# First-layer projections on one Trainium2 core: from one 32-bit matmul to three 16-bit matmuls, with GpSimd writing the arrangements

## The chip, the cores and the metric

The kernel runs on one core of a Trainium2 chip. The metric is device time in microseconds (us) of one execution, as the median of several. The engines are named as the profile names them: PE (TensorE, matmuls), PEld (TensorE's weight loads), DVE (VectorE), ACT (ScalarE), POOL (GpSimd), SP (SyncE, which issues the DMAs).

## The reference, cut to what matters

The network has several layers on x of shape (8, 128, 32, 32). The change lies in the first, a window attention with shifts 0 and 2, two channel halves and a local position term:

```python
for s in SHIFTS:                                   # (0, 2)
    xs = jnp.roll(x, (-s, -s), axis=(1, 2)) if s > 0 else x
    for idx, (nh, hs, nw, ws) in enumerate(strip_params):
        xsp = xs[:, idx * sd:(idx + 1) * sd]
        qkv = jnp.einsum('bchw,oc->bohw', xsp, wq)
        q, k, v = (qkv[:, :sd], qkv[:, sd:2 * sd], qkv[:, 2 * sd:])
        lepe = _dwconv3(v, w_lepe, b_lepe)         # 3x3 depthwise, per channel
        ...
        ow = jnp.einsum('whqk,whkc->whqc', attn, vw) + lw
```

Its input is x after a group norm, and x is added to its result.

## The kernel before, in words

All of this is the stage `window_projections` (line 205 on), one call, between the group norm's statistics and the stage `window_attention`, which reads what this stage stores. The stages are separated by a barrier of all engines. Channels lie on the 128 partitions, and a position of an image is a column (N = 1024, HALF = 512). The function `images` (L236) makes every engine walk the 8 images in order, two buffer slots in turn; within an image `u` counts four units (two shifts by two directions of strips), and each engine's instructions stand in the order in which its function is written. What one engine hands another goes over semaphores that count up; `grant` gives the buffers' first credits.

- **DVE** prepares an image one ahead (`prepare`, L276 to L280): it normalises X into `xn`, repeats its first 64 columns at the end, and copies it into `xw`, the same positions in the order of the vertical strips.
- **PE** makes for each unit the scores' projections (L332: two matmuls of 512 columns into `qk_ps`, all queries and keys of the unit) and the values (L337: eight matmuls of 64 columns into `v_ps`, with a block of 128 positions of the image as the stationary operand). Even units read `xw`, odd ones `xn`. After the four units the image's local position terms are summed in `l_ps` (L346): values and 3x3 taps are folded into one matrix for each tap (`wt`, made by DVE at the start), so a term is a matmul on the padded image `xp`, shifted by the tap; `lepe_pieces` cuts them at the image's edges into 36 pieces, 18 of one row (32 columns), 9 of 512 columns and 9 of 416 to 480. All of these operands are 32-bit, and one 32-bit matmul stands in the trace as two MATMUL records, each with its weight load.
- **ACT** casts each `qk_ps` to 16 bit (`hl`, L310), copies `v_ps` out (L313), and after the four units pads the next image into `xp` (L303).
- **DVE** subtracts the cast from `qk_ps` to get the low 16-bit half (L286), and after `l_ready` adds `l_ps` and the bias sum `bsum` to X (L291).
- **SP** stores both halves with four DMAs for each unit (`store_stacks`, L201 and L202) and the values with one (L254). `hl`, `vs`, `qk_ps` and `v_ps` have two buffers each: ACT may not write `hl` for a unit until the stores of the unit two before have landed (`hl_out`), and PE may not write `qk_ps` until DVE is through with the unit two before (`lo_done`).
- **POOL** does nothing in this stage.

At the stage's start SP loads the weights (L246) and the taps (L247); DVE waits for all five loads, makes `wt`, and only then normalises the first image.

The lines that the change and the prediction touch are those named above. `copy_scaled` (L360) is the copy by GpSimd, a multiplication by a column of ones.

Of the kernel before, what the change touches and what calls it, by code (L numbers as in the profile page):

```python
# [34 lines left out]
HALF = N // 2  # L35
D = 8
SHIFT = 16.0
STACK = 3 * D
ROWS = STACK + 2
MAX_UNIT = 32768.0  # L40
# [164 lines left out]
def window_projections(chip, X, mean_g, rstd_g, dram, qk_scr, v_scr):  # L205
# [4 lines left out]
    with chip.stage() as ctx:  # L210
# [6 lines left out]
        bsum = chip.buf(ctx, "bsum", [C, 1])  # L217
        scratch = chip.buf(ctx, "scratch", [1, 16])
        xn = chip.buf(ctx, "xn", [C, 2, N + 64])
        xw = chip.buf(ctx, "xw", [C, 2, N])  # L220
        xp = chip.buf(ctx, "xp", [C, 2, H, W + 2])
# [5 lines left out]
        w_loaded, weights, normed, padded, edge, strips = (chip.sem(s) for s in (  # L227
            "w_loaded", "weights", "normed", "padded", "edge", "strips"))
        qk_ready, hi_done, lo_done = (chip.sem(s) for s in ("qk_ready", "hi_done", "lo_done"))
        v_ready, v_copied, l_ready, l_added = (chip.sem(s) for s in ("v_ready", "v_copied", "l_ready", "l_added"))  # L230
        hl_out = [chip.sem("hl_out") for _ in range(2)]
        v_out = [chip.sem("v_out") for _ in range(2)]

# [8 lines left out]
        with nc.Block() as block:  # L242
            @block.sync
            def _(sp):
                for dst, name in ((wqk, "w0_qk"), (wv, "w0_v"), (wl, "w0_lepe"), (bl, "b_lepe")):
                    sp.dma_start(dst[:], dram[name]).then_inc(w_loaded, 16)  # L246
                sp.dma_start(taps[:].rearrange("p s t c -> p (s t c)"),  # L247
                             dram["lepe_taps"].to_broadcast([C, 2 * 9 * C])).then_inc(w_loaded, 16)
# [12 lines left out]
            def _(v):  # L261
                grant(nc, scratch, [(lo_done, 2), (v_copied, 2), (l_added, 1),
                                    (hl_out[0], 64), (hl_out[1], 64), (v_out[0], 16), (v_out[1], 16)])
                nc.vector.memset(xp[:], 0.0).then_inc(weights, 1)
                v.wait_ge(w_loaded, 16 * 5)
                nc.vector.tensor_scalar(wqk[:], wqk[:], SHIFT, None, ALU.mult).then_inc(weights, 1)
                for s in range(2):
                    nc.vector.tensor_tensor(wt[:, s], taps[:, s],
                                            wl[:, s].unsqueeze(1).to_broadcast([C, 9, C]), ALU.mult).then_inc(weights, 1)
                nc.vector.tensor_tensor(bsum[:], bl[:, 0:1], bl[:, 1:2], ALU.add).then_inc(weights, 1)  # L270
                v.wait_ge(weights, 5)
                nc.vector.tensor_tensor(wt[:, 2], wt[:, 0], wt[:, 1], ALU.add).then_inc(weights, 1)

                def prepare(i, slot):

                    nc.vector.tensor_scalar(xn[:, slot, 0:N], X[:, i, :], mean_g[:, i, :], rstd_g[:, i, :],  # L276
                                            ALU.subtract, ALU.mult).then_inc(normed, 1)
                    v.wait_ge(normed, i + 1)
                    nc.vector.tensor_copy(xn[:, slot, N:N + 64], xn[:, slot, 0:64]).then_inc(edge, 1)
                    nc.vector.tensor_copy(xw[:, slot].rearrange("p (n h w) -> p n h w", n=8, w=4),  # L280
                                          xn[:, slot, 0:N].rearrange("p (h n w) -> p n h w", n=8, w=4)).then_inc(strips, 1)
# [12 lines left out]
                prepare(0, 0)  # L294
                images(v, image)

            @block.scalar
            def _(act):
                act.wait_ge(weights, 1)

                def pad(i, slot):
                    act.wait_ge(normed, i + 1)
                    nc.scalar.copy(xp[:, slot, :, 1:W + 1],  # L303
                                   xn[:, slot, 0:N].rearrange("p (h w) -> p h w", h=H)).then_inc(padded, 1)

                def image(i, slot, last):
                    for u in range(U):
                        act.wait_ge(qk_ready, i * U + u + 1)
                        act.wait_ge(hl_out[u % 2], i * 128 + (u // 2 * 64 + 64))
                        nc.scalar.copy(hl[:, u % 2, 0], qk_ps[:, u % 2]).then_inc(hi_done, 1)  # L310
                        act.wait_ge(v_ready, i * U + u + 1)
                        act.wait_ge(v_out[u % 2], i * 32 + (u // 2 * 16 + 16))
                        nc.scalar.copy(vs[:, u % 2], v_ps[:, u % 2]).then_inc(v_copied, 1)  # L313
                    if not last:
                        pad(i + 1, 1 - slot)

                pad(0, 0)
                images(act, image)

            @block.tensor  # L320
            def _(pe):
                pe.wait_ge(weights, 6)
                def image(i, slot, last):
                    pe.wait_ge(strips, i + 1)
                    for u in range(U):
                        src = (xw if u % 2 == 0 else xn)[:, slot]
                        at = 64 if u == 3 else 0
                        if u == 1:
                            pe.wait_ge(edge, i + 1)
                        pe.wait_ge(lo_done, i * U + u + 1)  # L330
                        for c in range(2):
                            last = nc.tensor.matmul(qk_ps[:, u % 2, c * HALF:(c + 1) * HALF], wqk[:, u, :],  # L332
                                                    src[:, at + c * HALF:at + (c + 1) * HALF], start=True, stop=True)
                        last.then_inc(qk_ready, 1)
                        pe.wait_ge(v_copied, i * U + u + 1)
                        for w in range(8):
                            last = nc.tensor.matmul(v_ps[:, u % 2, w * 64:(w + 1) * 64],  # L337
                                                    src[:, at + w * C:at + (w + 1) * C], wv[:, u, :],
                                                    start=True, stop=True)
                        last.then_inc(v_ready, 1)  # L340
                    pe.wait_ge(padded, i + 1)
                    pe.wait_ge(l_added, i + 1)
                    for half in range(2):
                        pieces = lepe_pieces(half)
                        for n, (tap, kind, r, rows, r_in) in enumerate(pieces):
                            last = nc.tensor.matmul(  # L346
                                l_ps[:, r * W:(r + rows) * W], wt[:, kind, tap, :],
                                xp[:, slot, r_in:r_in + rows, tap % 3:tap % 3 + W],
                                start=(n == 0), stop=(n == len(pieces) - 1))
                    last.then_inc(l_ready, 1)  # L350

                images(pe, image)


# [1962 lines left out]
```

## Time and profile before

| | |
|---|---|
| time, median of 3 runs | 3906.41 us (3897.05 to 3911.96) |
| the profiled execution, its own time | 3902.64 us |
| its span in the trace, first to last instruction | 3900.8 us |
| mean granted TensorE clock over the span | 0.92 of full speed |
| busy over the span | PE 86%, DVE 70%, ACT 54%, POOL 26% |
| this stage in the trace | about 20 us to 300 us |

The profile is one execution taken by the hardware profiler. Times in its rows are microseconds from the start of the span, "x64" is a count of instructions, and the time in brackets is how long the engine had stood idle before and what released it. Matmuls overlap in the trace, so the time of one is not what it costs in a row of many: for that, the starts of two rows are subtracted. PEclk is the granted clock of TensorE as a share of its full speed.

### The profile page before, as it was taken

The numbers are of one execution on the slowest core, as the hardware profiler recorded it, in microseconds if no ns is written. First come the engines' busy times: TensorE is split into PE (matmuls) and PEld (weight loads), VectorE is DVE, ScalarE is ACT, GpSimd is POOL, SyncE is SP. The second block draws the span as 40 slices with busy tenths as digits, with TensorE's granted clock in tenths as the row PEclk, the third lists the DMA queues.
The fourth block names the chain that finished last, engine by engine and source line by source line (L and its number), as shares of the span: only waits on it lengthen the run. The fifth ranks groups of instructions, "written<-read, shape, count | busy, mean of one in ns | idle before, by whom it ended". The sixth has DMA issues, their size and how long they took to land. (4 is left out here: it accounts for less than half of the span.)

```text
span 3900.8 us, 68078 instructions
## 1 busy us (share of the span) xinstructions
PE 3362.7 (86%) x24815; PEld 1499.4 (38%) x24815; DVE 2734.7 (70%) x4437; ACT 2099.7 (54%) x2668; POOL 1000.6 (26%) x868
## 2 busy tenths in 40 slices
PE   6997778846779999999999999778987949999999
PEld 4664445523522222222222222163356734444444
DVE  3227767646479999999899999443449647777776
ACT  1224667711217777777777777633432325555555
POOL 0001343320000000000000000004420048888887
PEclk9997877868869999999999999979999859999999
DMA  4443555510320000000000100004410114323230
GB/s 149 129 130 85 114 119 117 106 20 0 118 79 16 21 18 25 16 22 21 21 22 16 27 16 16 11 11 151 151 48 0 45 46 114 100 81 101 89 93 27
DMA packets 137471, 243.06 MB, mean 62 GB/s; under 512 B 36776, under 2 KB 49232, under 8 KB 136720
## 3 DMA queue, kind: packets, MB, share of 16 engines
q1 hardware_dynamic: 137232, 239.79, 22.6%
q8 instruction: 160, 2.62, 0.3%
q14 instruction: 79, 0.65, 0.1%
HBM read 167.36 MB, written 56.62 MB: 57 GB/s over the span
## 5 line engine op out<-in xcount | busy, mean ns | idle before, releaser
L1075 DVE TENSOR_REDUCE mxv<-mx_ps 128x1 f32<-128x512 f32 x2048 | 1277.0, 683 | 90.1 <-PE mx_ps L934 71.9
L1050 ACT ACTIVATE PT<-st_ps 128x1024 f32<-128x1024 f32 x1024 | 997.1, 1022 | 297.5 <-PE st_ps L947 297.3
L934 PE MATMUL mx_ps<-KS,QS 24*128 24x512 f16 x2048 | 613.7, 394 | 113.8 <-DVE mxv L1075 96.4
L2024 POOL TENSOR_TENSOR hg<-u,gb 128x512 f32<-128x512 f32 x352 | 580.3, 1654 | 131.5 <-DVE u L1985 101.2
L961 PE MATMUL o_ps<-PT,VA 128*32 128x512 f32 x4096 | 550.9, 610 | 0.5 <-ACT PT L1050 0.5
L947 PE MATMUL st_ps<-QS,KS 26*128 26x512 f16 x2048 | 400.6, 388 | 9.2 <-ACT TX L1040 8.4
L669 DVE TENSOR_REDUCE mxv<-mx_ps 128x4 f32<-128x512 f32 x512 | 319.8, 684 | 122.4 <-PE mx_ps L544 118.1
L1985 DVE TENSOR_TENSOR u<-h_ps,s 128x512 f32<-128x512 f32 x352 | 243.1, 691 | 190.7 <-ACT s L1946 185.6
L1946 ACT ACTIVATE s<-h_ps 128x512 f32<-128x512 f32 x352 | 210.0, 596 | 284.0 <-PE h_ps L1901 284.0
L947 PEld LDWEIGHTS st_ps<-QS,KS 26*128 26x128 f16 x2048 | 96.5, 91 | 559.2 <-issue 481.6
L365 POOL TENSOR_TENSOR mt<-nm,less 128x16 f32<-128x16 f32 x64 | 13.8, 216 | 1113.9 <-DVE nm L1080 1113.9
L645 ACT ACTIVATE PT<-st_ps 128x1024 f32<-128x1024 f32 x256 | 253.0, 1030 | 72.4 <-PE st_ps L560 71.1
L1899 PE MATMUL h_ps<-xh,m_wh 128*128 128x512 f16 x704 | 268.5, 381 | 12.5 <-DVE xl L1968 8.9
L1900 PE MATMUL h_ps<-xl,m_wh 128*128 128x512 f16 x704 | 268.3, 381 | 0.0
L1901 PE MATMUL h_ps<-xs,m_wl 128*128 128x512 f16 x704 | 268.1, 381 | 0.0
L1974 DVE TENSOR_TENSOR hl<-hg,hh 128x512 f16<-128x512 f32 x352 | 257.3, 731 | 0.1
L934 PEld LDWEIGHTS mx_ps<-KS,QS 24*128 24x128 f16 x2048 | 142.7, 91 | 294.7 <-DVE mxv L1075 272.5
L365 POOL TENSOR_TENSOR VA<-VS,unit 128x512 f32<-128x512 f32 (+1 forms) x64 | 52.9, 826 | 646.1 <-DMA VS<-v 604.0
L1941 ACT CAST hh<-hg 128x512 f16<-128x512 f32 x352 | 214.8, 610 | 5.0 <-POOL hg L2024 4.8
L544 PE MATMUL mx_ps<-QK 24*128 24x128 f16 x2048 | 173.4, 245 | 34.5 <-DMA QK<-qk 18.3
L370 PE MATMUL st_ps<-KS,ident 128*128 128x512 f16 x512 | 201.2, 393 | 1.6 <-ACT PT L1050 0.9
L560 PE MATMUL st_ps<-QK 26*128 26x128 f16 x2048 | 118.0, 243 | 59.0 <-DMA QK<-mT 58.4
(237 smaller groups left out, 4747.2 us busy)
## 6 DMA issues: line engine op xcount, KB each, us to landing
gb<-g SPq DMA_DIRECT2D x64, 512.0 KB, 3.7
gb<-g SPq DMA_DIRECT2D x32, 1024.0 KB, 5.6
QK<-qk SPq DMA_DIRECT2D x128, 192.0 KB
qk<-hl SPq DMA_DIRECT2D x80, 256.0 KB, 3.3
RB<-d SPq DMA_DIRECT2D x48, 256.0 KB, 3.5
gb<-g SPq DMA_DIRECT2D x64, 192.0 KB, 5.7
qk<-hl SPq DMA_DIRECT2D x64, 128.0 KB, 3.2
v<-vs SPq DMA_DIRECT2D x32, 256.0 KB
```

The source lines that it names most:

```text
L645: nc.scalar.activation(PT[:, n % 2, 2 * a:2 * a + 2], st_ps[:, a], ACT.Exp, scale=SCALE).then_inc(st_free[a], 1)
L669: nc.vector.tensor_reduce(mxv[:, u % 2, j, n // 2 % 2, at:at + 4], mx_ps[:, slot].rearrange("p (w k) -> p w k", w=4), AX.X, ALU.max).then_ ...
L934: nc.tensor.matmul(mx_ps[:, use % 3, :], rows(QS, g // 2, j, STACK)[:, t * C:(t + 1) * C], rows(KS, g // 2, j, STACK)[:, half * HALF:(half ...
L947: mm = nc.tensor.matmul(st_ps[:, a, e], rows(KS, g // 2, 2 * a + e, ROWS)[:, kt * C:(kt + 1) * C], rows(QS, g // 2, 2 * a + e, ROWS)[:, g ...
L961: mm = nc.tensor.matmul(o_ps[32 * j:32 * j + 32, :], VA[:, g // 2 % 2, kt, j, :], PT[:, n % 2, j, :], start=(kt == 0), stop=(kt == KT - 1))
L1050: nc.scalar.activation(PT[:, n % 2, 2 * a:2 * a + 2], st_ps[:, a], ACT.Exp, scale=1.0 / SHIFT ** 2).then_inc(st_free[a], 1)
L1075: nc.vector.tensor_reduce(mxv[:, g % 2, j, t, half:half + 1], mx_ps[:, slot], AX.X, ALU.max).then_inc(mx_free, 1)
L1899: nc.tensor.matmul(out, wh[:, m, c, :], xh[:, s], start=True, stop=False)
L1900: nc.tensor.matmul(out, wh[:, m, c, :], xl[:, s], start=False, stop=False)
L1901: mm = nc.tensor.matmul(out, wl[:, m, c, :], xs[:, s], start=False, stop=True)
L1974: nc.vector.tensor_tensor(hl[:, n % PARTS], hg[:, n % HG_SLOTS], hh[:, n % PARTS], ALU.subtract).then_inc(low_part, 1)
L2024: nc.gpsimd.tensor_tensor(hg[:, n % HG_SLOTS], u[:, n % H_SLOTS], gb[:, s, tile], ALU.mult).then_inc(gated, 1)
```

## The change

Inputs, weights and tap matrices of this stage are split into a high 16-bit part (a cast) and a low one (whole minus high, cast). Each 32-bit matmul becomes three 16-bit ones into the same sum: high by high, high weight by low input, low weight by high input. Weights of the values and taps are scaled by 2^8, and ACT's copy of `v_ps` and DVE's addition of `l_ps` scale back. ACT makes the high parts of the next image (`high_parts`) between its two jobs of unit 1, DVE the low parts (`low_parts`) after its job of unit 1, and POOL writes the strip order and the padded image, of either part, and adds the bias to X. At the start the first image is normalised before the weights are there, PE begins when scores' and values' weights are split, and the taps' matrices are split before ACT's and DVE's first image.

```diff
+        wqk_h, wqk_l = (chip.buf(ctx, n, [C, 4, C], F16) for n in ("wqk_h", "wqk_l"))
+        wv_h, wv_l = (chip.buf(ctx, n, [C, 4, 64], F16) for n in ("wv_h", "wv_l"))
+        wt_h, wt_l = (chip.buf(ctx, n, [C, 3, 9, C], F16) for n in ("wt_h", "wt_l"))
...
             def _(v):
+                def low(n):
+                    whole, hi, lo = SPLIT[n]
+                    v.wait_ge(w_hi, n + 1)
+                    nc.vector.tensor_tensor(lo[:], whole[:], hi[:], ALU.subtract).then_inc(w_lo, 1)
...
+                def low_parts(i, slot):
+
+                    v.wait_ge(x_hi, i * 2 + 2)
+                    nc.vector.tensor_tensor(xl[:, slot, 0:N], xn[:, slot], xh[:, slot, 0:N], ALU.subtract).then_inc(x_lo, 1)
+                    nc.vector.tensor_tensor(xl[:, slot, N:N + 64], xn[:, slot, 0:64], xh[:, slot, 0:64],
+                                            ALU.subtract).then_inc(x_lo, 1)
...
                         if u == 0 and not last:
-                            prepare(i + 1, 1 - slot)
+                            normalise(i + 1, 1 - slot)
+                        if u == 1 and not last:
+                            low_parts(i + 1, 1 - slot)
                     v.wait_ge(l_ready, i + 1)
-                    nc.vector.scalar_tensor_tensor(X[:, i, :], l_ps[:], bsum[:], X[:, i, :],
-                                                   ALU.add, ALU.add).then_inc(l_added, 1)
+                    v.wait_ge(biased, i + 1)
+                    nc.vector.scalar_tensor_tensor(X[:, i, :], l_ps[:], 1 / V_SCALE, X[:, i, :],
+                                                   ALU.mult, ALU.add).then_inc(l_added, 1)
...
+                normalise(0, 0)
+                v.wait_ge(w_loaded, 16 * 4)
...
+                low_parts(0, 0)
+                low(0)
+                low(1)
+                v.wait_ge(scaled, 3)
+                v.wait_ge(taps_loaded, 16)
...
+                low(2)
                 images(v, image)
...
             def _(act):
+                def high_parts(i, slot):
+
                     act.wait_ge(normed, i + 1)
+                    nc.scalar.copy(xh[:, slot, 0:N], xn[:, slot]).then_inc(x_hi, 1)
+                    nc.scalar.copy(xh[:, slot, N:N + 64], xn[:, slot, 0:64]).then_inc(x_hi, 1)
...
+                high_parts(0, 0)
+                high(0, 1)
+                high(1, 2)
+                high(2, 6)
                 images(act, image)
+
+            @block.gpsimd
+            def _(pool):
+                def image(i, slot, last):
+
+                    for needs, flat, strip in ((x_hi, xh, xwh), (x_lo, xl, xwl)):
+                        pool.wait_ge(needs, i * 2 + 2)
+                        copy_scaled(nc, strip[:, slot].rearrange("p (n h w) -> p n h w", n=8, w=4),
+                                    flat[:, slot, 0:N].rearrange("p (h n w) -> p n h w", n=8, w=4), unit).then_inc(strips, 1)
+                    for flat, pad in ((xh, xph), (xl, xpl)):
+                        copy_scaled(nc, pad[:, slot, :, 1:W + 1],
+                                    flat[:, slot, 0:N].rearrange("p (h w) -> p h w", h=H), unit).then_inc(padded, 1)
+                    nc.gpsimd.tensor_tensor(X[:, i, :], X[:, i, :], bsum[:].to_broadcast([C, N]), ALU.add).then_inc(biased, 1)
...
             def _(pe):
...
+                        if u == 0:
+                            pe.wait_ge(strips, i * 2 + 2)
...
+                            nc.tensor.matmul(out, wqk_h[:, u, :], hi, start=True, stop=False)
+                            nc.tensor.matmul(out, wqk_h[:, u, :], lo, start=False, stop=False)
+                            mm = nc.tensor.matmul(out, wqk_l[:, u, :], hi, start=False, stop=True)
...
+                            nc.tensor.matmul(out, hi, wv_h[:, u, :], start=True, stop=False)
+                            nc.tensor.matmul(out, hi, wv_l[:, u, :], start=False, stop=False)
+                            mm = nc.tensor.matmul(out, lo, wv_h[:, u, :], start=False, stop=True)
...
+                    pe.wait_ge(w_lo, 3)
+                    pe.wait_ge(padded, i * 2 + 2)
...
+                            nc.tensor.matmul(out, wt_h[:, kind, tap, :], hi, start=(n == 0), stop=False)
+                            nc.tensor.matmul(out, wt_h[:, kind, tap, :], lo, start=False, stop=False)
+                            mm = nc.tensor.matmul(out, wt_l[:, kind, tap, :], hi, start=False, stop=(n == len(pieces) - 1))
```

On PE, one odd unit of an image before (a row with x2 or x8 is so many instructions):

```order
L332 MATMUL qk_ps<-xn,wqk 128x512 x2
L337 MATMUL v_ps<-wv,xn 128x64 x8
L330 REGISTER_ALU
L332 MATMUL qk_ps<-xw,wqk 128x512 x2
L337 MATMUL v_ps<-wv,xw 128x64 x8
```

and the same unit now, from its second half of the scores' projections to the first block of the values (xh and xl are the image's high and low part):

```order
L385 MATMUL qk_ps<-xh,wqk_h 128x512
L386 MATMUL qk_ps<-xl,wqk_h 128x512
L387 MATMUL qk_ps<-xh,wqk_l 128x512
L393 MATMUL v_ps<-wv_h,xh 128x64
L394 MATMUL v_ps<-wv_l,xh 128x64
L395 MATMUL v_ps<-wv_h,xl 128x64
```

So a unit has 6 and 24 matmuls where it had 2 and 8, and the last three rows repeat for each of the eight blocks of values.

On ACT, the start of the stage now (x's first image, the three weight tensors, then the first image's own work from the branch on); before, only the padding copy of the first image stood ahead of the branch:

```order
L332 CAST xh<-xn 128x1024
L333 CAST xh<-xn 128x64
L327 CAST wqk_h<-wqk 128x512
L327 CAST wv_h<-wv 128x256
L327 CAST wt_h<-wt 128x3456
L244 UNCONDITIONAL_BRANCH
L244 ISA
L338 ISA
L339 CAST hl<-qk_ps 128x1024
```

The cast of the taps' matrices, which waits for the taps, stands ahead of the first cast of `qk_ps`, and the same holds for DVE's subtraction of them.

## Rows read from the trace of the kernel before

**Rows 1.** The page, busy time of each engine, share of the span, instructions.

```profile
PE 3362.7 (86%) x24815; PEld 1499.4 (38%) x24815; DVE 2734.7 (70%) x4437; ACT 2099.7 (54%) x2668; POOL 1000.6 (26%) x868
```

**Rows 2.** By stretch, one image: length; busy PE, PEld, DVE, ACT, POOL; PEclk; DMA.

```profile
68.50:101.00 32.50, 32.50 (x155) 20.99 (x153) 7.70 (x8) 7.21 (x9) 0.00 (x0) 1.00 0.47 130
```

**Rows 3.** Groups, 0 to 420 us: busy and mean ns, then idle before, releasers.

```profile
L286 DVE TENSOR_TENSOR hl<-qk_ps,hl 128x1024 f16<-128x1024 f32 x32 | 39.2, 1225 | 72.8 <-ACT hl L310 72.8
L332 PE MATMUL qk_ps<-xw,wqk 128*128 128x512 f32 x64 | 33.0, 640 | 15.6 <-DVE xw L280 15.6
L310 ACT CAST hl<-qk_ps 128x1024 f16<-128x1024 f32 x32 | 32.4, 1012 | 176.0 <-PE qk_ps L332 137.4 <-DMA qk<-hl 38.6
...
L313 ACT COPY vs<-v_ps 128x512 f32<-128x512 f32 x32 | 18.8, 588 | 12.7 <-PE v_ps L337 11.8 <-DMA v<-vs 0.9
...
L303 ACT COPY xp<-xn 128x1024 f32<-128x1024 f32 x8 | 8.5, 1059 | 14.4 <-DVE xn L276 14.4
...
L268 DVE TENSOR_TENSOR wt<-taps,wl 128x1152 f32<-128x1152 f32 x2 | 2.6, 1352 | 0.0
```

**Rows 4.** PE in order of time, second image: start, us, line, tiles, count.

```profile
68.51 1.96 PE L332 MATMUL qk_ps<-xw,wqk 128*128 128x512 f32 x4
70.31 1.89 PE L337 MATMUL v_ps<-wv,xw 128*128 128x64 f32 x16
...
82.55 18.65 PE L346 MATMUL l_ps<-xp,wt 128*128 128x512 f32 x72
101.04 1.96 PE L332 MATMUL qk_ps<-xw,wqk 128*128 128x512 f32 x4
```

**Rows 5.** Busy by stretch in a later stage whose matmuls are 16-bit, 512 columns.

```profile
3300.00:3500.00 200.00, 200.00 (x928) 90.60 (x927) 148.47 (x216) 118.24 (x217) 170.03 (x104) 1.00 0.33 96
```

**Rows 6.** 16-bit matmuls of 128 columns: two bursts and four in a row, by time.

```profile
375.78 0.23 PE L560 MATMUL st_ps<-QK 26*128 26x128 f16 x2
...
375.98 0.23 PE L544 MATMUL mx_ps<-QK 24*128 24x128 f16 x2
...
377.09 0.39 PE L544 MATMUL mx_ps<-QK 24*128 24x128 f16 x4 [0.21 <-DVE mxv L669]
```

**Rows 7.** The tile mx_ps, 330 to 960 us: ns of one, min/median/max.

```profile
L544 PE MATMUL mx_ps<-QK x1945: 211/214/309, 329.7 to 768.2; 24*128 24x128 f16 x195
```

**Rows 8.** PE by time: 32-bit passes of 1 and of 128 columns.

```profile
968.47 1.84 PE L1378 MATMUL v_ps<-mean_w,sq 128*128 128x1 f32 x16
970.17 2.03 PE L1388 MATMUL r_ps<-identf,rs 128*128 128x128 f32 x16
972.04 1.88 PE L1370 MATMUL m_ps<-X,mean_w 128*128 x4
```

**Rows 9.** All engines by time, the stage's start and its last image's end.

```profile
21.60 0.43 SPq L247 DMA_DIRECT2D taps<-in_lepe_taps  x1
27.79 0.43 DVE L266 TENSOR_SCALAR wqk<-wqk 128x512 f32<-128x512 f32 x1 [5.39 <-DMA taps<-in_lepe_taps]
...
33.92 3.78 PE L332 MATMUL qk_ps<-xw,wqk 128*128 128x512 f32 x4 [15.62 <-DVE xw L280]
...
38.86 1.23 DVE L286 TENSOR_TENSOR hl<-qk_ps,hl 128x1024 f16<-128x1024 f32 x1 [5.08 <-ACT hl L310]
...
296.40 1.28 DVE L291 SCALAR_TENSOR_TENSOR X<-l_ps,bsum,X 128x1024 f32<-128x1024 f32 x1 [16.53 <-PE l_ps L346]
```

**Rows 10.** SP's queue and ACT by time, second image: stores and the wait for them.

```profile
73.06 0.65 SPq L201 DMA_DIRECT2D qk<-hl  x1
...
78.76 1.01 ACT L310 CAST hl<-qk_ps 128x1024 f16<-128x1024 f32 x1 [2.42 <-DMA qk<-hl]
...
81.19 0.64 SPq L201 DMA_DIRECT2D qk<-hl  x1
```

**Rows 11.** POOL's groups over the whole run: busy and mean ns, idle before.

```profile
L2024 POOL TENSOR_TENSOR hg<-u,gb 128x512 f32<-128x512 f32 x352 | 580.3, 1654 | 131.5 <-DVE u L1985 101.2 <-DMA gb<-g 28.2
...
L746 POOL TENSOR_TENSOR ON<-ON,RB 128x1024 f32<-128x1024 f32 x16 | 37.6, 2348 | 101.6 <-DMA RB<-d 80.5 <-DMA ON<-OR 21.1
```

More of the change, by code:

```diff
@@ L37 @@
 SHIFT = 16.0
+V_SCALE = 2.0 ** 8
 STACK = 3 * D
@@ L261, in _, with normalise @@
             def _(v):
[L262 to L276, printed above, removed]
-                                            ALU.subtract, ALU.mult).then_inc(normed, 1)
[L278 to L281, printed above, removed]
+                def low(n):
+                    whole, hi, lo = SPLIT[n]
+                    v.wait_ge(w_hi, n + 1)
+                    nc.vector.tensor_tensor(lo[:], whole[:], hi[:], ALU.subtract).then_inc(w_lo, 1)
+                def normalise(i, slot):
+                    nc.vector.tensor_scalar(xn[:, slot], X[:, i, :], mean_g[:, i, :], rstd_g[:, i, :],
+                                            ALU.subtract, ALU.mult).then_inc(normed, 1)
+                def low_parts(i, slot):
[3 more added lines that the diff above has]
+                                            ALU.subtract).then_inc(x_lo, 1)
                 def image(i, slot, last):
@@ L298, in _, with high @@
             def _(act):
[L299 to L301 removed]
+                def high(n, needs):
+                    whole, hi, _ = SPLIT[n]
+                    act.wait_ge(scaled, needs)
+                    nc.scalar.copy(hi[:], whole[:]).then_inc(w_hi, 1)
+                def high_parts(i, slot):
                     act.wait_ge(normed, i + 1)
[L303 to L304 removed]
+                    nc.scalar.copy(xh[:, slot, 0:N], xn[:, slot]).then_inc(x_hi, 1)
+                    nc.scalar.copy(xh[:, slot, N:N + 64], xn[:, slot, 0:64]).then_inc(x_hi, 1)
                 def image(i, slot, last):
@@ L310, in image @@
                         nc.scalar.copy(hl[:, u % 2, 0], qk_ps[:, u % 2]).then_inc(hi_done, 1)
+                        if u == 1 and not last:
+                            high_parts(i + 1, 1 - slot)
                         act.wait_ge(v_ready, i * U + u + 1)
                         act.wait_ge(v_out[u % 2], i * 32 + (u // 2 * 16 + 16))
-                        nc.scalar.copy(vs[:, u % 2], v_ps[:, u % 2]).then_inc(v_copied, 1)
-                    if not last:
-                        pad(i + 1, 1 - slot)
@@ L317, in _ @@
-                pad(0, 0)
-                images(act, image)
+                        nc.scalar.activation(vs[:, u % 2], v_ps[:, u % 2], ACT.Copy, scale=1 / V_SCALE).then_inc(v_copied, 1)
+                high_parts(0, 0)
+                high(0, 1)
+                high(1, 2)
+                high(2, 6)
+                images(act, image)
+            @block.gpsimd
[9 more added lines that the diff above has]
+                    nc.gpsimd.tensor_tensor(X[:, i, :], X[:, i, :], bsum[:].to_broadcast([C, N]), ALU.add).then_inc(biased, 1)
+                for pad in (xph, xpl):
+                    nc.gpsimd.memset(pad[:], 0.0).then_inc(cleared, 1)
+                pool.wait_ge(cleared, 3)
+                pool.wait_ge(bias_ready, 1)
+                images(pool, image)
@@ L330, in image @@
                         pe.wait_ge(lo_done, i * U + u + 1)
                         for c in range(2):
-                            last = nc.tensor.matmul(qk_ps[:, u % 2, c * HALF:(c + 1) * HALF], wqk[:, u, :],
-                                                    src[:, at + c * HALF:at + (c + 1) * HALF], start=True, stop=True)
-                        last.then_inc(qk_ready, 1)
+                            out = qk_ps[:, u % 2, c * HALF:(c + 1) * HALF]
+                            hi, lo = (x[:, slot, at + c * HALF:at + (c + 1) * HALF] for x in flat)
@@ L345, in image @@
                         for n, (tap, kind, r, rows, r_in) in enumerate(pieces):
[L346 to L350, printed above, removed]
+                            out = l_ps[:, r * W:(r + rows) * W]
+                            hi, lo = (x[:, slot, r_in:r_in + rows, tap % 3:tap % 3 + W] for x in (xph, xpl))
+                            nc.tensor.matmul(out, wt_h[:, kind, tap, :], hi, start=(n == 0), stop=False)
+                            nc.tensor.matmul(out, wt_h[:, kind, tap, :], lo, start=False, stop=False)
+                            mm = nc.tensor.matmul(out, wt_l[:, kind, tap, :], hi, start=False, stop=(n == len(pieces) - 1))
+                    mm.then_inc(l_ready, 1)
+                pe.wait_ge(w_lo, 2)
                 images(pe, image)
```

46 lines of the change are left out of this document (29 added, 17 removed).

## Prediction

> **What bounds the kernel now.** I read the page first. PE is busy for 86% of the span [rows 1], but that is a mean over stages with different limits, so the next view is the stretch of one image of this stage, 68.5 to 101.0 us. There PE is busy for the whole 32.50 us at PEclk 1.00 (the 2.4 GHz level), DVE for 7.70 us, ACT for 7.21 us and POOL for nothing [rows 2]. The groups agree: PE's only idle time before a line of this stage is the 15.6 us before its first matmul, while ACT and DVE wait for PE and for each other, and ACT for stores (38.6 us) [rows 3]. So inside the stage time is PE's work and nothing else. In order of time an image is four units of 3.51 us (68.51 to 82.55), each 1.80 us of scores' projections and 1.71 us of values, and 18.49 us of position terms (82.55 to 101.04): 32.53 us in all [rows 4]. Eight such images are 260 us of 3902.64.
>
> **What PE's new work costs.** The 16-bit stream of a later stage has 928 matmuls of 512 columns in 200.00 us, with a fresh weight load for each: 0.2155 us apiece at PEclk 1.00 [rows 5]. The loads cost nothing there.
> - Scores: 4 units x 6 matmuls = 24 x 0.2155 = 5.17 us, for 4 x 1.80 = 7.2.
> - Position terms, large pieces: 9 x 3 = 27 of 512 columns, 5.82 us; 27 of 416 to 480, by their mean of 448 columns 0.189 each, 5.09 us. Together 10.91.
> - Small ones: 4 x 8 x 3 = 96 of 64 columns (values) and 18 x 3 = 54 of 32 columns (image edges). No row shows a 16-bit matmul of so few columns with full weights, so I bound it. From above: four matmuls of 128 columns, each with its own 128-column load in the same array rows, take 0.39 us, of which one's own time is 0.214 [rows 6, 7]; (0.39 - 0.214) / 3 = 0.059 each. From below: columns alone, 64/512 and 32/512 of 0.2155, are 0.027 and 0.0135; issuing is no floor above that, as 14 such matmuls start between 375.78 and 375.98 us, 0.014 each [rows 6]. I take 0.030 for both, near the lower row, because in the row of four the load hides behind the matmul and the load of 16-bit weights should be well under its 0.059. That gives 150 x 0.030 = 4.5 us; the ends are 3.3 and 8.9.
>
> An image is then 5.17 + 10.91 + 4.5 = 20.58 us (19.4 to 24.9), against 32.53.
>
> **Who else could set that pace.**
> - ACT: four casts of 1.012, four copies of 0.588, high parts as the padding copy's 1.059 plus some 0.2 for the edge [rows 3]: 7.7 us. Between unit 1's two jobs these 1.3 us delay its value copy, and PE's values of unit 3 wait for that copy; they come two units (4 us) later, so it is covered.
> - DVE: 4 x 1.225, normalising (0.8, unchanged), low parts by the 1152-element tensor operation's 1.352 about 1.2 plus 0.2 [rows 3], adding 1.28 [rows 9]: 8.4 us. The strip copy (0.7) goes to POOL.
> - POOL, five passes of 1024 elements, 2.35 us each by the quiet row, 3.3 by the row beside a busy DVE (1.654 for 512) [rows 11]: 11.8 to 16.5 us. It starts when the low part exists, about 7 us into the image before; strips are done by 14 us (wanted at 20.6), padding by 20.5 (wanted 8 us into the next image), the bias by 24 (DVE wants it at 41). Behind POOL's waits stands only its own next pass.
> - Stores: unchanged in number. A buffer's turn, from one unit's first store to that of the unit two later, is 81.19 - 73.06 = 8.13 us, the cast at 78.76 having waited for landing [rows 10]. Two buffers, four units: 16.3 us an image, which 32.5 hid easily and 20.6 still hides. This is next in line, and the reason why less than 16.3 cannot be had.
>
> **The start.** Before, the taps' landing released DVE at 27.79, PE began at 33.92 and DVE's first subtraction ran at 38.86 [rows 9]. Now weights without taps (issued before the taps at 21.60, landed by 27.79; I take 24) let DVE scale and split, and POOL's two strip copies (4.7 to 6.6 us) let PE begin at about 30, half-clocked at first, as the first four records' 3.78 us against 1.96 show for now [rows 9, 4]. That lead is lost again: the taps' matrices take DVE 3 x 1.352 from 27.79 (to 31.9), ACT's cast of 3456 columns about 3.2 (from 0.588 for 512 and 1.059 for 1024 [rows 3]; to 35.1), DVE's subtraction 3 x 1.352 (to 39.2), and only then does DVE take unit 0 (to 40.4). PE stands from about 35 to 40.5, and its units 2 and 3 cost 4.0 us and some 2 more if the clock has fallen meanwhile. Position terms begin at 46.6 and last 10.91 + 1.62 = 12.5: image 0 ends at 59.1, where it ended at 68.51 [rows 4].
>
> **The sum.** 59.1 + 7 x 20.58 = 203.2 us for PE's end, which was about 296.2 (DVE's last addition starts at 296.40 [rows 9]): 93.0 us earlier. The last unit's stores land some 22 us after its image began, half a microsecond after DVE is done, so 92.5 remain. Nothing later changes. 3902.64 - 92.5 = 3810.1; the profiled execution lies 3.8 under the median of the runs shown, so I say 3812. At 0.059 the sum is 48.0 + 14.1 + 7 x 24.9 = 236.4, 60 us less than 296.2, or 3843; at the lower end it is near 3802.
>
> **Rivals.**
> - *The load is not hidden behind small matmuls.* 32-bit passes of 1 column take (970.17 - 968.47) / 16 = 0.106 us and those of 128 columns 0.117 [rows 8]: there the weights set the pace and columns are free. Values before cost 1.71 / 16 = 0.107 a pass [rows 4]. If a 16-bit load cost as much, 150 x 0.107 = 16.1 and an image 32.1; the start brings a few us, the end comes near 292, and the time is about 3898, no change: three small matmuls for two small passes eat what the large ones give. Against it stands 0.059 for load and matmul together [rows 6, 7]. Chance 0.10, half of it at the full price, half between this and my forecast.
>  The Trainium skill (TensorE: Matmul & The Clock Gate, Back-to-back issue gap) gives about 81 ns a matmul at 128 columns where each has its load; by that, kept for 64 and 32 columns, an image would be 28.2 us and the time an estimated 3869, within that half. The trace disagrees with its figure: 59 ns.
> - *POOL becomes the bound.* The strip copies read runs of 4 elements of 2 bytes; no row shows that. Above 4.1 us a pass POOL sets the image's time, above about 6.7, twice the slowest row per element (3.2 ns) [rows 11], the stage is slower than before: at 8 us an image is 40, the last one's strips come at 24.5 + 7 x 40 + 16 = 320, its terms end near 349, and the time is about 3955. For it: nothing but the unseen access. Chance 0.05 (slower 0.02, no change 0.01, a smaller gain 0.02).
> - *The granted clock falls.* At the 1.2 GHz level an image would be 41 us and the stage 60 us longer, near 3965. The later 16-bit stage stood at PEclk 1.00 with PE full [rows 5], and PE is full here. Chance 0.03, with one in three for slower, mostly a partial fall that takes some of the gain.
>
> **How the numbers follow.** The forecast has the remaining 0.82. Its range is 3797 to 3850: prices of the small matmuls give 3802 to 3843, the runs' own spread (about 7 us to either side of their median) the rest; what is left outside is the rivals and a start that I have mis-timed. A measurement of this kernel can tell about 0.5%, 19.5 us, from no change. Faster: 0.82, half of 0.10, and 0.04 from POOL and clock, 0.91. Same: 0.05 and 0.01, 0.06. Slower: 0.02 and 0.01, 0.03.
>
> **What would show it.** In the profile after: image to image about 20.6 us on PE, with PE busy throughout; scores' units of 1.29 us, values' of 0.7 (1.4 at the upper price); terms of 12.5; PE starting near 30 and standing from 35 to 40 for DVE; POOL's passes of 2.3 to 3.3 us; the stage's end near 204. I am wrong if PE shows idle time before unit 0 (POOL's strips late) or unit 2 and 3 (stores late) in later images, if values take 2.5 us a unit, or if pieces of the padded image, whose 16-bit rows start at odd places, cost more than their columns.

## The result, and the profile after

| | before | changed |
|---|---|---|
| median of 4 runs, us (lowest to highest) | 3906.40 (3897.05 to 3911.96) | 3811.16 (3808.28 to 3815.21) |
| the profiled execution, us | 3902.64 | 3811.67 |
| its span, us | 3900.8 | 3809.9 |
| mean granted clock of the span | 0.920 | 0.918 |
| end of the stage's last matmul, us | 296.36 | 210.45 |

The ratio is 0.9759, with a 95% interval of 0.9738 to 0.9780: faster, by 95 us between the medians. The forecast was 3812.

The page's line of the engines and, below it, two stretches of the changed kernel. The columns of the second fence are length; busy time of PE, PEld, DVE, ACT and POOL with their instructions; PEclk; DMA share; GB/s.

```profile
PE 3264.2 (86%) x25423; PEld 1424.5 (37%) x25423; DVE 2763.9 (73%) x4442; ACT 2104.2 (55%) x2679; POOL 1091.3 (29%) x910
```

```profile
20.00:66.80 46.80, 25.06 (x229) 13.83 (x230) 30.02 (x28) 12.22 (x15) 27.36 (x12) 0.89 0.44 126
66.80:87.30 20.50, 20.50 (x233) 11.75 (x231) 9.88 (x8) 7.23 (x10) 10.38 (x5) 1.00 0.66 174
```

PE's share of the whole is 86% as before [rows 1] and tells nothing. The second stretch is one image, the answer to [rows 2]: 20.50 us where there were 32.50, PE still busy for all of it at PEclk 1.00, and POOL's five passes take 10.38 us in its shadow. The first stretch is the start with image 0: PE worked for only 25.06 of its 46.80 us. So the stage is still PE's in every later image, and at the start it is not.

PE's timeline of the changed kernel shows both (start, duration, engine, line, operation; in brackets the idle time before it and what ended it):

```profile
31.34 0.61 PE L385 MATMUL qk_ps<-xwh,wqk_h 128*128 128x512 f16 x1 [12.88 <-DVE wv_l L273]
...
36.70 0.19 PE L393 MATMUL v_ps<-wv_h,xh 128*128 128x64 f16 x1
36.73 0.19 PE L394 MATMUL v_ps<-wv_l,xh 128*128 128x64 f16 x1
36.76 0.19 PE L395 MATMUL v_ps<-wv_h,xl 128*128 128x64 f16 x1
...
47.97 0.61 PE L385 MATMUL qk_ps<-xwh,wqk_h 128*128 128x512 f16 x1 [10.40 <-DVE hl L289]
...
54.24 0.39 PE L405 MATMUL l_ps<-xph,wt_h 128*128 128x512 f16 x1
...
56.23 0.18 PE L405 MATMUL l_ps<-xph,wt_h 128*128 128x32 f16 x1
56.25 0.18 PE L406 MATMUL l_ps<-xpl,wt_h 128*128 128x32 f16 x1
56.28 0.18 PE L407 MATMUL l_ps<-xph,wt_l 128*128 128x32 f16 x1
```

Over a unit's 24 matmuls, those of 64 columns start 29 ns apart on average, and those of 32 columns 25 ns apart, each with its own weights: the duration of 0.18 or 0.19 us that a row prints is pipelined, so the distance of starts is the price. But PE stood for 10.40 us ahead of unit 2 of image 0, until DVE's `hl`, and its terms began at 54.24 where 46.6 was forecast. After this wait it worked at the 1.2 GHz level for a while: from 47.90 to 52.00 PEclk is 0.50 and matmuls of 512 columns start 0.43 us apart, later 0.215. From 31.34 to 35.6 they start 0.43 us apart as well, although PEclk reads 1.00 there.

Where the time came from, in the two profiled executions: PE's work of the stage ends 85.9 us earlier (296.40 to 210.48, where DVE's last addition starts), and what lies behind it is 5.0 us shorter, 90.9 us of span together. These are the stretches behind the stage, before and changed (columns as above):

```profile
296.40:3900.80 3604.40, 3099.11 (x23595) 1329.30 (x23595) 2655.96 (x4329) 2040.72 (x2594) 1000.39 (x864) 0.91 0.21 56
```

```profile
210.50:3809.90 3599.40, 3094.33 (x23595) 1327.38 (x23595) 2656.49 (x4329) 2040.97 (x2594) 1001.36 (x864) 0.92 0.21 57
```

The same 23595 matmuls, 5 us apart; the forecast had taken this stretch as unchanged, apart from half a microsecond of stores. So the total came out right by luck in part, for it hides two differences: a start that came 7.6 us later than forecast, and 5 us that came from somewhere else. The experiments take these two first, and then the sum's other terms.

Who held PE up at the start is to be read from the timeline of DVE, POOL and ACT there:

```profile
20.24 2.18 DVE L276 TENSOR_SCALAR xn<-X,mean_g,rstd_g 128x1024 f32<-128x1024 f32 x1
...
25.80 2.47 POOL L424 TENSOR_TENSOR xwh<-xh,unit 128x1024 f16<-128x1024 f16 x1 [1.53 <-DVE bsum L308]
26.43 1.92 DVE L283 TENSOR_TENSOR xl<-xn,xh 128x64 f16<-128x64 f32 x1
28.43 2.27 POOL L424 TENSOR_TENSOR xwl<-xl,unit 128x1024 f16<-128x1024 f16 x1 [0.16 <-DVE xl L283]
28.87 2.11 DVE L273 TENSOR_TENSOR wv_l<-wv,wv_h 128x256 f16<-128x256 f32 x1
30.66 2.07 POOL L424 TENSOR_TENSOR xph<-xh,unit 128x1024 f16<-128x1024 f16 x1
30.91 6.01 DVE L315 TENSOR_TENSOR wt<-taps,wl 128x1152 f32<-128x1152 f32 x2
32.70 3.00 POOL L424 TENSOR_TENSOR xpl<-xl,unit 128x1024 f16<-128x1024 f16 x1
35.66 3.00 POOL L363 TENSOR_TENSOR X<-X,bsum 128x1024 f32 x1
36.95 2.93 DVE L318 TENSOR_TENSOR wt<-wt 128x1152 f32<-128x1152 f32 x1
39.91 3.07 ACT L327 CAST wt_h<-wt 128x3456 f16<-128x3456 f32 x1 [14.04 <-DVE wt L318]
43.02 3.76 DVE L273 TENSOR_TENSOR wt_l<-wt,wt_h 128x3456 f16<-128x3456 f32 x1 [3.14 <-ACT wt_h L327]
46.69 1.22 DVE L289 TENSOR_TENSOR hl<-qk_ps,hl 128x1024 f16<-128x1024 f32 x1
```

DVE's three products of the taps (the third is their sum) take 3.04, 3.04 and 2.93 us where the same operation took 1.352 alone [rows 3], a subtraction of 64 columns takes 1.92, and a subtraction of 256 columns 2.11. Each of these reads two operands from SBUF. POOL's pass `xwh` is over at 28.27 and the 64-column subtraction at 28.35; `xph` is over at 32.73 and the first product about 1.2 us later, its own time; the third product is over at 39.88, 1.22 after POOL's bias pass (38.66). POOL waits in the same way: `xpl` and the bias pass take 3.00 us each, of which 1.9 is what a pass needs later in the stage and the rest a product's end to wait for. `hl`, which reads PSUM, takes its 1.22 us whenever it runs: in a later image two of its four run beside POOL's passes, and the 32 of the stage have a mean of 1.224. So POOL's passes and DVE's operations on two SBUF operands take turns, a whole instruction at a time. The Trainium skill (SBUF — State Buffer, SBUF: two separate sides) has this as a rule: a GpSimd operation that reads SBUF and a VectorE operation with two SBUF inputs share a pair of ports, which whichever starts first holds for its whole instruction while the other stands. The trace agrees, 1.92 us for 64 columns that need 0.22 alone (experiment 2). The prediction had not drawn on it. Operations with two SBUF tensors are not the only ones: the normalising into `xn`, with one, took 2.18 us beside POOL's clearing of `xph` (19.97 to 21.88) and takes 0.80 in a later image. That wait cost nothing, since the weights landed later (24.48).

### The profile page after: what moved, and what is told of

Its sections match the earlier page's. It is cut to its first block and busy times, and to the rows that moved or that the text cites. A ratio compares the mean times of both kernels' runs of the same rounds, so it can differ in the third digit from the quotient of the medians.

```text
span 3809.9 us, 69393 instructions
## 1 busy us (share of the span) xinstructions
PE 3264.2 (86%) x25423; PEld 1424.5 (37%) x25423; DVE 2763.9 (73%) x4442; ACT 2104.2 (55%) x2679; POOL 1091.3 (29%) x910
## 5 line engine op out<-in xcount | busy, mean ns | idle before, releaser
L632 PE MATMUL o_ps<-PT,VA 128*32 128x128 f32 x4096 | 166.2, 311 | 2.7 <-issue 1.5
```

## Experiments

Times are compared with runs of the kernel before on the same chip: the first four kernels with 7 runs (median 3901.99 us), the other three with 9 (median 3907.09). A kernel with a single execution has one time and no interval; there the profile's stage times carry the argument, since they hardly differ between executions: image to image is 20.50 us in five kernels, and the stage's last matmul ended at 210.45 and 210.85 us in two executions of the changed one. DVE's first instruction of the stage, though, starts between 19.24 and 20.11 us in the eight executions with 16-bit matmuls (20.03 in the changed kernel's first), so a difference of less than a microsecond between two of them is not given a cause.

**1. pool_holds: POOL waits until DVE has made the taps' matrices.** One line in POOL's part, ahead of the two padded copies (6 is the count of `scaled` that DVE's third product reaches):

```diff
+                    pool.wait_ge(scaled, 6)
                     for flat, pad in ((xh, xph), (xl, xpl)):
```

> One wait added: in each image GpSimd starts the padded copies only when the taps' products exist (a wait that is over at once from the second image on). In the changed kernel DVE's products took 3.04 us and 2.93 us each where the same operations took 1.35 us before, and its 64-column subtraction 1.9 us. Theory (a DVE operation with two SBUF inputs waits until the GpSimd pass that is running is over): the three products take 1.35 us each again, 4.1 us instead of 8.9, PE's first position terms start 3 to 5 us earlier than 54.24 us, its last matmul ends at 205.5 to 207.5 us instead of 210.4, and an image stays at 20.37 us. Rival (the products are slow because the taps are still landing or because of their operands): they stay near 3 us, the stage's end stays at 210 us or moves later by what the padded copies are late.

Measured: 3803.95 us, one execution. The groups of this run at the start (line, engine, operation, count, then busy time, mean ns of one, idle before):

```profile
L315 DVE TENSOR_TENSOR wt<-taps,wl 128x1152 f32<-128x1152 f32 x2 | 2.6, 1346 | 0.0
L318 DVE TENSOR_TENSOR wt<-wt 128x1152 f32<-128x1152 f32 x1 | 1.4, 1358 | 0.0
L283 DVE TENSOR_TENSOR xl<-xn,xh 128x64 f16<-128x64 f32 x3 | 5.7, 1913 | 0.0
```

The products are back at 1346 and 1358 ns with nothing but POOL held off, while the 64-column subtraction, beside which POOL's strip copy still runs, keeps its 1913. The three take 4.0 us instead of 9.0, so sharing is the cause of those 5.0 us. The terms begin at 49.33 instead of 54.24 and the last matmul ends at 205.53 instead of 210.45, 4.9 us earlier, with the image at 20.50. Of these 4.9 us the wait itself gave 4.0: in this execution the products also began 0.9 us earlier, at 29.99, where the wait had not yet acted, and two later steps gave back 0.5 and 0.4. The first of them is the sharing again, as POOL's bias pass and DVE's subtraction now meet:

```profile
37.14 4.30 DVE L273 TENSOR_TENSOR wt_l<-wt,wt_h 128x3456 f16<-128x3456 f32 x1 [3.14 <-ACT wt_h L327]
37.78 5.41 POOL L364 TENSOR_TENSOR X<-X,bsum 128x1024 f32 x1
```

The second is units 2 and 3, 6.70 us instead of 6.27. What this run leaves is the late begin of the products: their taps' landing would release them at 27.88, as experiment 2 shows.

**2. no_gpsimd: the whole of POOL's part given to DVE and ACT.** DVE writes the strips and adds the bias, ACT writes the padded copies, and POOL's block goes:

```diff
+                    for flat, strip in ((xh, xwh), (xl, xwl)):
...
+                        nc.vector.tensor_copy(strip[:, slot].rearrange("p (n h w) -> p n h w", n=8, w=4),
...
+                            nc.vector.tensor_scalar(X[:, i, :], X[:, i, :], bsum[:], None, ALU.add).then_inc(biased, 1)
...
+                    for flat, dst in ((xh, xph), (xl, xpl)):
+                        nc.scalar.copy(dst[:, slot, :, 1:W + 1],
...
-            @block.gpsimd
-            def _(pool):
...
```

> GpSimd's part undone: DVE writes the strip order after the low parts and adds the bias to X after unit 2, ACT writes the two padded copies after unit 3 as before the change; the three 16-bit matmuls stay. Theory (PE's work sets the image's time, so who writes the arrangements does not matter once an image is done ahead): image to image 20.4 us as now, DVE some 10 us and ACT some 10 us of it; at the start DVE is not slowed, its first low half of unit 0 ends near 41 us instead of 47.9, the stage's last matmul ends near 204 us, and the time is that of the changed kernel or up to 7 us less (3804 to 3812 us). Rival (the gain needs GpSimd to take copies off DVE and ACT): an image takes 21.5 us or more and the time is 3820 us or more.

Measured: 3811.64 us median of 4 (3806.94 to 3833.18), ratio 0.9787 (0.9745 to 0.9829). Its groups at the start, its first two products in the timeline, and one image:

```profile
L283 DVE TENSOR_TENSOR xl<-xn,xh 128x64 f16<-128x64 f32 x3 | 0.7, 219 | 0.0
L288 DVE COPY xwl<-xl 128x1024 f16<-128x1024 f16 x3 | 1.3, 421 | 0.0
L273 DVE TENSOR_TENSOR wv_l<-wv,wv_h 128x256 f16<-128x256 f32 x1 | 0.4, 418 | 0.0
```

```profile
27.88 2.63 DVE L323 TENSOR_TENSOR wt<-taps,wl 128x1152 f32<-128x1152 f32 x2 [0.20 <-DMA taps<-in_lepe_taps]
```

```profile
58.10:78.60 20.50, 20.50 (x233) 11.74 (x231) 9.52 (x11) 9.12 (x12) 0.00 (x0) 1.00 0.71 189
```

The same subtractions cost 219 and 418 ns instead of 1.92 and 2.11 us, and a strip copy 421 ns on DVE against 1.9 on POOL. PE begins at 28.04, the terms at 45.55, and the last matmul ends at 201.75, 8.7 us before the changed kernel's. Half a microsecond of that is this execution's, whose stage began at 19.54 instead of 20.03. In the steady images DVE and ACT do it all inside the same 20.50 us: the "GpSimd writing the arrangements" of the change gives nothing here, and its cost is about 8 us of the start. In the run's time this can't be seen (the interval of the ratio is 0.84% of the time wide, 33 us); it is read from the trace's stage times.

**3. two_products: every third matmul left out.** What is left out is the product with the low weight part, everywhere in the stage:

```diff
-                            nc.tensor.matmul(out, wqk_h[:, u, :], lo, start=False, stop=False)
-                            mm = nc.tensor.matmul(out, wqk_l[:, u, :], hi, start=False, stop=True)
+                            mm = nc.tensor.matmul(out, wqk_h[:, u, :], lo, start=False, stop=True)
```

and likewise for values and taps.

> Every product with a low weight part is left out (two 16-bit matmuls where there are three), so part of the sums is missing. PE's work for an image falls from 20.37 to 13.6 us. Theory (the stores' ring is next, 8.1 us for a buffer's turn, two buffers, four units, 16.3 us): an image takes 16.3 to 17.5 us, PE stands before units 2 and 3 or before the next image's units until DVE's low half of the unit two before is done, and the stage's last matmul ends near 176 to 184 us. Rival (nothing else is near, the next bound is GpSimd at 10.4 or DVE at 10 us): 13.6 us an image and the end near 156 us.

Measured: 3784.76 us, one execution; the last matmul ends at 182.94. One image of it, ACT's group over 60 to 185 us, and one of ACT's casts in its timeline:

```profile
96.00:114.10 18.10, 13.95 (x154) 7.87 (x153) 9.81 (x8) 7.13 (x10) 10.35 (x6) 1.00 0.89 243
```

```profile
L339 ACT CAST hl<-qk_ps 128x1024 f16<-128x1024 f32 x28 | 28.3, 1012 | 74.2 <-DMA qk<-hl 59.1 <-PE qk_ps L386 15.0
```

```profile
71.75 1.01 ACT L339 CAST hl<-qk_ps 128x1024 f16<-128x1024 f32 x1 [2.81 <-DMA qk<-hl]
```

PE has 13.95 us of work in a stretch of 18.10 and stands for the rest. ACT waits 59.1 us for the scores' stores to land before it may write a buffer again. So the stores through the ring of two buffers are the next bound, as the prediction said, at a mean image of 17.84 us (six images from 60.71 to 167.72); the forecast of 16.3 from one turn of the ring [rows 10] was 1.5 too low. The same stretch has a DMA share of 0.89 against 0.66 in the changed kernel's image above; whether the number of buffers or the DMA engines set the 17.84 was not tried.

**4. values_32bit: only the values put back.** One 32-bit matmul for each three:

```diff
-                            nc.tensor.matmul(out, hi, wv_h[:, u, :], start=True, stop=False)
-                            nc.tensor.matmul(out, hi, wv_l[:, u, :], start=False, stop=False)
-                            mm = nc.tensor.matmul(out, lo, wv_h[:, u, :], start=False, stop=True)
+                            mm = nc.tensor.matmul(out, whole, wv[:, u, :], start=True, stop=True)
```

(DVE keeps a 32-bit strip copy for it.)

> The values alone go back to one 32-bit matmul (with their own 32-bit input in strip order, copied by DVE); scores and position terms stay in three 16-bit ones. Theory (inside the stage only PE's work counts and its parts add up): a unit's values cost 1.71 us again instead of 0.70, an image 20.37 + 4 x 1.01 = 24.4 us, the stage's last matmul ends near 240 us, the time is near 3841 us. Rival (the small matmuls are not what the gain hangs on, or something else hides them): an image at 20.4 to 21.5 us and the end near 211 to 220 us.

Measured: 3839.20 us, one execution; last matmul at 241.13. One image:

```profile
68.60:93.20 24.60, 24.60 (x200) 16.22 (x199) 10.61 (x10) 7.23 (x10) 10.42 (x5) 1.00 0.63 171
```

24.60 against 20.50: the 64-column values alone are worth 4.1 us an image. That is what the parts say: four units of 1.71 us before [rows 4] against four of 0.70. Three 16-bit matmuls beat the two 32-bit passes even at 64 columns: a 32-bit pass takes 0.107 us there and 0.106 with a single column [rows 8], so its columns do not set its price, while a 16-bit matmul, with a fresh load of as many weights, starts every 0.029 us.

**5. changed_again: the changed kernel, unedited, five more times.** It asks whether the later stages are faster because of the change.

> The changed kernel itself, on the chip and beside the rounds of the two kernels below, for the spread of the stages that the change does not touch. Theory (all of the change's gain lies in this stage; the stages behind it vary by some us from execution to execution): the stage ends at 210 us as before in the trace, the later stages differ from those of the first profile by up to 6 us in sum, the ratio is 0.976 again. Rival (later stages are faster because of the change): the window attention takes 475 us again and not the 481 us of the kernel before.

Measured: 3820.59 us median of 5 (3808.26 to 3824.09), ratio 0.9774 (0.9754 to 0.9794). Behind the stage's last matmul, by this run's stretches:

```profile
210.90:3813.70 3602.80, 3099.40 (x23595) 1331.07 (x23595) 2656.23 (x4329) 2041.35 (x2594) 1000.73 (x864) 0.91 0.21 57
```

3602.8 us with the same program that had 3599.4. In the other kernels, whose later stages are the same instructions, the stretch takes 3596.3 (values_32bit) to 3607.6 us (late_tap_split), and before it took 3604.4. The 5 us lie inside this spread of 11, which the same instructions show; what sets it in an execution is left open. The rival, that the change speeds up something later, falls. The window attention, from its first `mx_ps` matmul to its last of `st_ps`, took 475.9 us before and 471.4 in the changed kernel's first execution, but 474.1 here and 476.3 in late_tap_split. The five times of this run go with their granted clocks (0.917 for the two shortest, 0.913 and 0.909 for the two longest), which no run tests as a cause.

**6. late_tap_split: DVE and ACT take unit 2's work before the taps'.** POOL's wait of experiment 1, and the taps' split moved behind unit 1's work of image 0, so that the second half of image 0's scores does not stand behind it (the first two images are taken out of the loop for this):

```diff
+                        if u == 1 and type(i) is int and i == 0:
+                            low(2)
...
-                low(2)
...
+                        if u == 1 and first:
+                            high(2, 6)
+                            high_parts(i + 1, 1 - slot)
...
-                high(2, 6)
...
+                    pool.wait_ge(scaled, 6)
```

> The taps' matrices are split later, after the first image's second unit on ACT and DVE (the first two images stand outside the loop for it), and GpSimd starts its padded copies when the products exist. Theory (PE stands from 37.4 to 48.0 us because DVE's and ACT's first work on an image is queued behind the taps): PE's gap before unit 2 closes to under 2 us, the position terms start near 45 us instead of 54.2, the stage's last matmul ends near 201 us, an image stays at 20.5 us, and the time is some 9 us under the changed kernel's, about 3802 us, at the edge of what a measurement can tell. Rival (PE would wait anyway, for stores or for the split itself): the terms start at 50 us or later, the end is at 206 us or later.

Measured: 3807.34 us median of 5 (3803.80 to 3811.48), ratio 0.9742 (0.9727 to 0.9756). PE takes all four units without a stop (units start at 30.62, 34.45, 36.45 and 38.45), stands for 3.7 us before the terms, which begin at 44.28, and ends at 202.06, within about a microsecond of what was expected. That is 8.4 us before the changed kernel's end, 0.8 of it because this execution's stage began at 19.24.

**7. no_gpsimd_late_split: 2 and 6 together.**

```diff
+                    for flat, strip in ((xh, xwh), (xl, xwl)):
...
+                        if u == 1 and type(i) is int and i == 0:
+                            low(2)
...
-            @block.gpsimd
...
```

> GpSimd's part undone as in the run of that kind, and the taps' matrices split after the first image's second unit. Theory (both delays of the start add up, and GpSimd is not needed): terms start near 42.5 us, an image stays at 20.5 us, the last matmul ends near 198.5 us, the time is 10 to 12 us under the changed kernel's, near 3800 us. Rival (ACT's padding in the first image or DVE's strips make the first unit late): the end is at 203 us or later and the time is that of the changed kernel.

Measured: 3802.26 us median of 5 (3801.44 to 3814.73), ratio 0.9745 (0.9726 to 0.9764). Its unit 2 in PE's timeline, and one image:

```profile
34.17 0.38 PE L391 MATMUL qk_ps<-xwh,wqk_h 128*128 128x512 f16 x1
```

```profile
56.10:76.60 20.50, 20.50 (x232) 11.75 (x231) 9.53 (x11) 9.11 (x12) 0.00 (x0) 1.00 0.66 176
```

PE begins at 27.99, reaches unit 2 with no idle time before it at 34.17 (changed kernel: 47.97 after 10.40 us of waiting), the terms at 41.99, and ends at 199.79: 10.7 us before the changed kernel, 10.5 if both are counted from their stage's start, of which 8.2 are experiment 2's. It has the lowest median of all versions that compute the whole result, 18 us under the changed kernel's on the same chip, of which the trace accounts for 10.7; the intervals of the two ratios overlap (0.9726 to 0.9764 and 0.9754 to 0.9794), so the times alone do not settle it.

## Why the prediction was right, and where it was not

**The image: right, with two small misses that cancel.** 20.58 us were forecast and 20.50 measured. By parts: scores 1.29 us a unit, as said; values 0.70, as said; terms 12.52, as said (12.5). The price that no row showed, that of the small matmul, was 0.029 (64 columns) and 0.025 (32) against the chosen 0.030. At 64 columns that is near the lower of the two bounds, as argued: by the distance of starts the load hides. At 32 it is almost twice the lower bound of 0.0135, so the 0.014 between starts of other matmuls [rows 6] did not carry over to these. Ninety-six at 0.029 and 54 at 0.025 are 4.1 us, against 4.5. The terms still took 12.52, because one of the prediction's signs of being wrong came true in small: pieces of the padded image that start at an odd place cost more than their columns. The first two pieces of the second image's terms show it. The one is the middle tap, which starts one element into a padded row, and the other a tap that starts at a row's first element:

```profile
74.75 0.39 PE L405 MATMUL l_ps<-xph,wt_h 128*128 128x512 f16 x1
74.98 0.39 PE L406 MATMUL l_ps<-xpl,wt_h 128*128 128x512 f16 x1
75.21 0.39 PE L407 MATMUL l_ps<-xph,wt_l 128*128 128x512 f16 x1
75.44 0.38 PE L405 MATMUL l_ps<-xph,wt_h 128*128 128x512 f16 x1
75.65 0.38 PE L406 MATMUL l_ps<-xpl,wt_h 128*128 128x512 f16 x1
```

The three of the middle tap take 0.23 us each, the next 0.215. The same holds for all six large pieces of the taps of the middle column and for no other, 11 to 14 ns a matmul in the mean of seven images (0.229 against 0.216 at 512 columns, 0.186 against 0.175 at 416). Eighteen such matmuls are 0.23 us an image, as much as the small matmuls of the terms came under their forecast. That the sum of the terms was hit is luck; no run tries another padding.

**The rivals fell in the way they were written.** A load that isn't hidden would have given 32.1 us an image; PE's rows 25 to 29 ns apart rule it out, and values_32bit shows the 32-bit price and the 16-bit one side by side. The Trainium skill (TensorE: Matmul & The Clock Gate, Back-to-back issue gap) has two answers here. Its sustained figures with a load each, 81 ns at 128 columns and 131 ns at 512, do not hold: 512 columns take 215.5 ns. What it calls the isolated gap, columns / 2.4 + 2.5 ns with a floor of about 25, gives 29.2, 25 and 215.8 for 64, 32 and 512 columns, and the stage's stream of load and matmul shows just that, but for the pieces at odd places. Whether issue or the load sets the 25 ns was not tried. POOL did not become the bound: 10.38 us an image against the 11.8 to 16.5 that were reckoned; the strips' runs of four elements cost nothing (1.942 us against 1.919 for the padding's). The clock stayed at PEclk 1.00 in every image from the second on. In the first it was low at times, as forecast: PEclk 0.62 over units 2 and 3.

**The store ring: right as the next bound, too low in size.** With a third of PE's work gone an image takes 17.8 us, not 16.3. It did not touch the forecast, since 20.5 is above both.

**The start: wrong by 7.6 us, and the step is "DVE 3 x 1.352 from 27.79".** The order of events was as told: PE begins after the strips, stands for the taps' matrices, and DVE then takes unit 0. Two sizes in it were off. The products began at 30.91, since DVE was late with the subtractions ahead of them (64 columns 1.92 us instead of 0.22, 256 columns 2.11 instead of 0.42), 3.1 us; and they ended at 39.88, 9.0 us later instead of 4.1, 4.9 us. ACT's cast (3.07, forecast 3.2), DVE's subtraction (3.76, forecast 4.06) and units 2 and 3 (47.97 to 54.24, 6.27 us, forecast 6.1) were sized right, so the delay went through to the terms: 54.24 against 46.6. The prediction gave POOL the price "beside a busy DVE" from [rows 11] and did not ask the converse, what DVE pays beside a busy POOL. Shown by pool_holds (the products' 5.0 us back by one wait, 4.0 of them at the terms) and no_gpsimd (terms at 45.55, 1 us before the forecast).

**The tail: off by a microsecond.** PE stands for 19.79 us between the stage's last matmul and the first of the window attention, against 18.33 before: 1.5 us more, where half a microsecond was forecast. This is PE's first matmul behind the stage, before and changed (the bracket is the idle time and the load that ended it):

```profile
314.69 0.63 PE L544 MATMUL mx_ps<-QK 24*128 24x128 f16 x12 [18.33 <-DMA QK<-qk]
```

```profile
230.24 0.64 PE L603 MATMUL mx_ps<-QK 24*128 24x128 f16 x12 [19.79 <-DMA QK<-qk]
```

**The sum.** Start +7.6, seven images of 20.50 instead of 20.58 -0.6, tail +1.0: with these put right the prediction's sum, 3810.1 for the profiled execution, would have been 3818. The profiled execution says 3811.67, since behind the stage it was 5.0 us shorter than the one of before, where the tail alone would have made it 1.5 longer; the five executions of changed_again have their median at 3820.59. The range, 3797 to 3850, took in either.

## What to carry to other kernels

Price a change of number format by what an engine pays for an instruction of each size, and not by its columns alone: at 64 columns three 16-bit matmuls at 29 ns replaced two 32-bit passes at 107 ns, at 512 three at 215.5 ns replaced two at 450 [rows 4], so the change gained more on 64 columns (1.71 to 0.70 us a unit) than on 512 (1.80 to 1.29). Where work is given to an idle engine, read the other way round as well: what the engines that share its memory pay in the stretch where they set the pace. A total that hits to a microsecond is no proof of its terms: compare stage by stage, and measure how far unchanged stages wander (here 3596 to 3608 us) before a few microseconds are given a cause.

## What was not expected of the hardware

- A POOL pass and a DVE operation with two SBUF operands take turns for a whole instruction: 64 columns took 1.92 us instead of 0.22, products of 1152 elements 3.0 instead of 1.35, and POOL's passes 3.00 instead of 1.9. `hl`, with an operand in PSUM, kept 1.22.
- A 16-bit matmul with fresh weights costs 29 ns at 64 columns, near the 27 that columns alone would be by 215.5 ns for 512, but still 25 ns at 32, where they would be 13.5.
- The large 16-bit matmuls of the terms that start one element into a padded row cost 11 to 14 ns more than those that start at its first or third (0.229 instead of 0.216 us at 512 columns).
- A strip copy of 1024 16-bit elements takes 0.42 us on DVE and 1.9 on POOL.
